# Cross-attention of a fused attention and expert kernel, reassociated: scores from x̂ (Wq Kᵀ), output from P (V Wo)

## The reference

```python
xn  = layernorm(x)
q, k, v = xn @ Wq, ctx @ Wk, ctx @ Wv          # 8 heads of 64, inner width 512
P   = softmax(q k^T * 64**-0.5)                # per head, 256 x 77
x   = x + (P v) @ Wo + bo
h   = layernorm(x)
rw  = routing weights of 16 experts, from h @ normalized sim_matrix, gates, relu, top-2 fallback, softmax
q2, k2, v2 = sum over e of rw[e] * (h @ proj[e])   # 64 wide each, 16 experts
a   = causal softmax(q2 k2^T / 8) v2
out = x + sum over e of rw[e] * (a @ o_proj[e])
```

## Time and profile before

| | |
|---|---|
| median of 3 runs | 2771.4 us (2769.01 to 2772.56) |
| the profiled execution | 2767.65 us, of it a span of 2765.9 us from first to last instruction |
| busy share of the span | PE 98%, PEld 93%, DVE 81%, ACT 44%, POOL 43% |
| granted TensorE clock | 0.992 on average |
| DMA | 113.6 MB, 41 GB/s; the queue's packets take 16.9% of the 16 engines' time |
| chain that ended last | PE 90%, ACT 4%, DVE 2%, issue 2% |

### The profile page before, as it was taken

One profiled execution on the slowest core, in us unless ns is written; L12 is line 12 of the kernel. 1 busy time (PEld: TensorE's weight loads), 2 busy tenths in 40 slices (PEclk: granted clock), 3 DMA queues, 4 the chain that ended last, 5 costly groups with the idle time before them and its releaser, 6 DMA issues.

```text
span 2765.9 us, 65910 instructions
## 1 busy us (share of the span) xinstructions
PE 2698.9 (98%) x19012; PEld 2582.4 (93%) x19012; DVE 2233.7 (81%) x6371; ACT 1226.8 (44%) x4240; POOL 1186.2 (43%) x1739
## 2 busy tenths in 40 slices
PE   5999999999999999999999999999999999999996
PEld 4999999999999999999999999999999999999996
DVE  6788888888888888888888878888888888888875
ACT  4444444444444444544444444444445444444441
POOL 1353443444444444534434434444445344344343
PEclk8999999999999999999999999999999999999998
DMA  4111111111111111111111111211111111111111
GB/s 105 29 46 43 33 44 35 41 44 28 44 48 28 44 44 32 44 44 32 44 39 37 44 28 44 48 28 44 45 32 44 44 32 44 42 34 44 33 39 39
DMA packets 131437, 113.59 MB, mean 41 GB/s; under 512 B 24720, under 2 KB 130640, under 8 KB 131408
## 3 DMA queue, kind: packets, MB, share of 16 engines
q1 hardware_dynamic: 131408, 113.23, 16.9%
HBM read 95.38 MB, written 17.83 MB: 41 GB/s over the span
## 4 chain that ended last, share of the span: by engine, by line
PE 90%; ACT 4%; DVE 2%; issue 2%; POOL 0%; DMA 0%; DVEq 0%; ACTq 0%; SPq 0%; POOLq 0%
PE bank_b L373 12%; PE bank_b L374 11%; PE bank_b L375 11%; PE bank_a L375 10%; PE bank_a L374 10%; PE bank_a L373 10%; PE bank_c L373 5%; PE bank_c L375 5%; PE bank_c L374 5%; PE bank_a L487 4%; PE bank_c L551 1%; PE bank_a L447 1%; PE bank_a L446 1%; PE bank_a L418 1%; DVE k_stack L1011 1%
## 5 line engine op out<-in xcount | busy, mean ns | idle before, releaser
L373 PE MATMUL bank_b<-wqkv_hi,x2T_lo 128*128 128x384 f32 (+1 forms) x2048 | 719.8, 351 | 0.0
L374 PE MATMUL bank_b<-wqkv_lo,x2T_hi 128*128 128x384 f32 (+1 forms) x2048 | 693.8, 339 | 0.0
L375 PE MATMUL bank_b<-wqkv_hi,x2T_hi 128*128 128x384 f32 (+1 forms) x2048 | 688.7, 336 | 0.0
L1000 DVE SCALAR_TENSOR_TENSOR acc<-bank_b,rw,acc 128x192 f32<-128x192 f32 x1792 | 641.1, 406 | 4.9 <-PE bank_b L375 2.4
L1256 POOL TENSOR_TENSOR mixs_lo<-mix,mixs_hi 128x512 fp32r<-128x512 f32 x256 | 380.5, 1517 | 156.4 <-ACT mixs_hi L777 156.4
L373 PEld LDWEIGHTS bank_b<-wqkv_hi,x2T_lo 128*128 128x128 f32 x2048 | 386.1, 189 | 17.6 <-DVE acc L1000 17.2
L374 PEld LDWEIGHTS bank_b<-wqkv_lo,x2T_hi 128*128 128x128 f32 x2048 | 386.2, 189 | 0.0
L375 PEld LDWEIGHTS bank_b<-wqkv_hi,x2T_hi 128*128 128x128 f32 x2048 | 385.2, 188 | 0.0
L1178 POOL TENSOR_TENSOR pow_out<-pow_in,expo 128x2 f32<-128x2 f32 (+1 forms) x128 | 111.7, 873 | 607.6 <-DVE pow_in L862 508.3
L723 ACT ACTIVATE probs<-bank_a,s_max 128x77 f32<-128x77 f32 x1024 | 316.5, 330 | 56.6 <-DVE s_max L931 56.6
L373 PE MATMUL bank_c<-wo_hi,mixs_lo 128*128 128x256 f32 x1024 | 293.8, 287 | 3.7 <-POOL mixs_lo L1256 3.7
(11 more groups left out here) (195 smaller groups left out, 6926.9 us busy)
## 6 DMA issues: line engine op xcount, KB each, us to landing
rw_all<-rw_dram SPq DMA_DIRECT2D x128, 512.0 KB, 5.9
xt<-in_x_dram SPq DMA_DIRECT2D x64, 256.0 KB, 2.7
out_dram<-mix SPq DMA_DIRECT2D x64, 256.0 KB, 2.2
ct<-in_ctx_dram SPq DMA_DIRECT2D x64, 57.8 KB
ct<-in_ctx_dram SPq DMA_DIRECT2D x64, 19.2 KB
mix<-in_L_ffn_o_proj_dram SPq DMA_DIRECT2D x2, 512.0 KB, 4.4
rw_dram<-rwT SPq DMA_DIRECT2D x64, 16.0 KB, 1.4
x_tiles<-in_L_xattn_Wq_dram SPq DMA_DIRECT2D x1, 512.0 KB, 6.8
```

The source lines that it names most:

```text
L373: nc.tensor.matmul(dst, lhs[1], rhs[0], start=start, stop=False)
L374: nc.tensor.matmul(dst, lhs[0], rhs[1], start=False, stop=False)
L375: return nc.tensor.matmul(dst, lhs[0], rhs[0], start=False, stop=stop)
L1000: V.scalar_tensor_tensor(acc[:, t, k, :], src, rw[:, t, e:e + 1], acc[:, t, k, :], ALU.mult, ALU.add).then_inc(b_evac, 1)
```

## The change

Scores: S = xn (Wq Kᵀ). For each head G = Wq_h K_hᵀ (256 channels by 77 keys) is made ahead, and `a_s` multiplies the transposed xn by it; queries are no longer made. Output: y = P (V Wo). For each head U = V_h Wo_h (77 by 256), stacked to 616 rows; the normalized probabilities are transposed as 616 rows (five chunks of at most 128: 10 transposes) and multiplied by U in 30 matmuls; `a_pv` is gone. G and U depend on the context alone. They are made for three batches at once (231 key columns, padded to 232): one `j_ct`, 4 `j_k`, 4 `j_v`, 8 `j_g`, 8 `j_u` per group of three, spread over the three steps of a group by the table JOBS, and are written, hi and lo, to DRAM (`g_dram`, `u_dram`) through two `draft` tiles. Before its use each batch loads its G (128 rows of 9,856 bytes) and its U (616 rows of 2,048 bytes). Batch 0 is a group of its own, made in an opening before the first step; the group of batches 1 to 3 is made in the two steps of index -1 (17 jobs) and in the step of batch 0 (8 jobs).

The loop body is now three steps (r = 0, 1, 2). Several tiles share memory: xn and x2n lie in `probs`, `rwT` in `mix`, k_hi, q_stack, k_stack, v2, p2T in the two pT tiles, aT2 in the qkv part of `late_tiles`. POOL's order of pieces is unchanged. The diff, cut to its core:

```diff
+    A_ORDER = ("E0", "PT0", "PT1", "PT2", "E1", "Y", "E2", "E3", "M1", "XT", "M2", "M3", "S0", "S1", "S2", "S3", "L1", "L2")
+    JOBS = ({"E0": ("v", 2), "E1": ("u", 2), "E2": ("u", 3), "E3": ("v", 3), "M1": ("u", 4), "M2": ("u", 5), "M3": ("u", 6),
+             "L1": ("u", 7)},
+            {"E0": ("ct", 0), "E1": ("k", 0), "E2": ("k", 1), "E3": ("g", 0), "M1": ("g", 1), "M3": ("k", 2), "L1": ("g", 2),
+             "L2": ("g", 3)},
+            {"E0": ("k", 3), "E1": ("g", 4), "E2": ("g", 5), "E3": ("v", 0), "M1": ("g", 6), "M2": ("g", 7), "M3": ("v", 1),
+             "L1": ("u", 0), "L2": ("u", 1)})
...
 SP, new order of a step
+                if on(earlier):
+                    store(earlier)
+                turn((store_u, 2), (None,), (store_g, 4))
+                turn((store_u, 3), (None,), (store_g, 5))
+                turn((None,), (store_g, 0), (None,))
+                if r and on(ahead):
+                    load_u(ahead, q + 1, r)
+                turn((store_u, 4), (store_g, 1), (store_g, 6))
+                turn((store_u, 5), (None,), (store_g, 7))
+                if r == 1 and going(gm + 1):
+                    load_ctx(gm + 1)
+                if on(before):
+                    spread_rw(before)
...
 PE
+            def j_g(gm, f):
+                hc, cc = f // 2, f % 2
...
+                for e in range(2):
+                    dst, w_ = bank_job(gm, "g", f)[:, e * KP:e * KP + keys.stop], wq[:, 2 * hc + e, cc * P:(cc + 1) * P]
+                    nc.tensor.matmul(dst, w_, both[:, hc % 2, e, keys], start=True, stop=False)
+                    last = nc.tensor.matmul(dst, w_, only[:, hc % 2, e, keys], start=False, stop=True)
...
             def a_s(n, j):
+                for cc in range(CC):
+                    last = product(bank_a(f"S{j}")[:, 0:HB * NC].rearrange("p (a b) -> p a b", a=2),
+                                   part(xT, slice(None), cc, slice(t * P, (t + 1) * P)),
+                                   [gq[:, 2 * half:2 * half + 2, cc, k, :] for k in range(2)], cc == 0, cc == CC - 1)
+            def a_pT(n, k):
+                if k == 0:
+                    pe.wait_ge(p_ready, at(2, n, 1))
...
                 do(before, b_qkv, 6)
+                turn("E0", (j_v, 2), (j_ct,), (j_k, 3))
                 do(before, b_qkv, 7)
                 do(earlier, c_y, 0)
                 do(before, b_qkv, 8)
                 do(earlier, c_y, 1)
+                fill("PT0", now, a_pT, 0)
+                fill("PT1", now, a_pT, 1)
                 do(earlier, c_y, 2)
+                fill("PT2", now, a_pT, 2)
                 do(earlier, c_y, 3)
                 do(before, b_qkv, 9)
+                turn("E1", (j_u, 2), (j_k, 0), (j_g, 4))
                 do(before, b_qkv, 10)
+                fill("Y", now, a_y, 0)
                 do(before, b_qkv, 11)
+                turn("E2", (j_u, 3), (j_k, 1), (j_g, 5))
+                do(now, a_y, 1)
                 do(before, b_qkv, 12)
+                turn("E3", (j_v, 3), (j_g, 0), (j_v, 0))
                 do(before, b_qkv, 13)
                 do(before, b_qkv, 14)
                 do(before, b_qkv, 15)
+                turn("M1", (j_u, 4), (j_g, 1), (j_g, 6))
+                fill("XT", ahead, a_xT)
                 do(before, c_rT)
                 do(now, b_xT, 0)
                 do(now, b_xT, 1)
+                turn("M2", (j_u, 5), (None,), (j_g, 7))
                 do(before, c_qk)
                 do(now, b_qkv, 0)
                 do(now, b_qkv, 1)
                 do(before, c_s)
+                turn("M3", (j_u, 6), (j_k, 2), (j_v, 1))
                 do(now, b_qkv, 2)
+                fill("S0", ahead, a_s, 0)
+                fill("S1", ahead, a_s, 1)
+                fill("S2", ahead, a_s, 2)
                 do(before, c_pT)
+                do(now, b_qkv, 3)
                 do(before, c_pv)
+                fill("S3", ahead, a_s, 3)
                 do(now, b_qkv, 4)
+                turn("L1", (j_u, 7), (j_g, 2), (j_u, 0))
                 do(now, b_qkv, 5)
+                turn("L2", (None,), (j_g, 3), (j_u, 1))
...
 ACT, second half of a step
                 do(before, c_qk)
+                turn((j_u, 6), (j_k, 2), (j_v, 1))
                 do(before, c_exp)
                 do(now, b_exp)
+                do(ahead, a_exp, 0)
                 do(before, c_pT)
+                do(ahead, a_exp, 1)
                 do(before, c_pv)
+                do(ahead, a_exp, 2)
                 do(before, c_mix, 0)
+                do(ahead, a_exp, 3)
                 do(before, c_mix, 1)
+                turn((j_u, 7), (j_g, 2), (j_u, 0))
                 do(before, c_mix, 2)
+                turn((None,), (j_g, 3), (j_u, 1))
+                do(before, c_mix, 3)
...
 DVE, second half of a step
+                turn((j_u, 6), (j_k, 2), (j_v, 1))
+                do(ahead, a_s, 0)
                 do(before, c_p)
+                do(ahead, a_s, 1)
                 do(now, b_wsum)
+                do(now, b_qkv, 0)
+                do(ahead, a_s, 2)
                 do(before, c_pT)
                 do(now, b_qkv, 1)
                 do(now, b_qkv, 2)
+                do(now, b_qkv, 3)
                 do(before, c_mix, 0)
+                do(ahead, a_s, 3)
+                do(now, b_qkv, 4)
                 do(before, c_mix, 1)
+                turn((j_u, 7), (j_g, 2), (j_u, 0))
                 do(before, c_mix, 2)
+                turn((None,), (j_g, 3), (j_u, 1))
                 do(before, c_mix, 3)
```

More of the change, by code:

```diff
@@ L360, in _, with step, turn, skip @@
[L360 to L365, removed]
+            load_weights(range(0, 1))
+            load_x(0)
+            load_weights(range(1, 4))
+            load_ctx(1)
+            load_weights(range(4, 6))
+            def step(q, r):
+                ahead, now, before, earlier = [number(q, r) + d for d in (1, 0, -1, -2)]
+                after = number(q, r) + 2
+                gm = group(q, r)
+                def turn(*jobs):
+                    fn, *k = jobs[r]
+                    if fn and going(gm):
+                        fn(gm, *k)
+                def skip():
+                    pass
+                if on(earlier):
[11 more added lines that the diff above has]
+                    spread_rw(before)
+                if on(after) and not (known(after) and after == 0):
+                    load_x(after)
+                turn((store_u, 6), (None,), (None,))
+                if on(after):
+                    load_g(after, *((q + 1, r + 1) if r < 2 else (q + 2, 0)))
+                turn((store_u, 7), (store_g, 2), (store_u, 0))
+                turn((None,), (store_g, 3), (store_u, 1))
+                if not r and on(ahead):
+                    load_u(ahead, q + 1, r)
@@ new lines, in _ @@
+            for hc, pieces in enumerate(((6,), (7, 8), (9,), (10, 11))):
+                store_g(0, 2 * hc)
+                store_g(0, 2 * hc + 1)
+                load_weights(pieces)
+            for hc, pieces in enumerate(((12,), (13,), (), (14, 15))):
+                store_u(0, 2 * hc)
+                load_weights(pieces)
+            step(-1, 1)
+            step(-1, 2)
+            for r in range(3):
+                step(0, r)
+            with sp.Fori(1, LAST) as q:
+                for r in range(3):
+                    step(q, r)
@@ L366, in _ @@
+            for q, r in ENDING:
+                step(q, r)
             sp.wait_ge(y_out, 16 * B)
@@ L503, in a_y @@
[L503 to L511 removed]
+                last.then_inc(xt_fill, 1)
@@ new lines, in j_u @@
+            def j_u(gm, f):
+                hc, tile = f // 2, f % 2
+                weights(gm, W_O)
+                pe.wait_ge(kv_evac, at(H, gm, HC + hc))
+                keys = slice(0, NC) if opened(gm) else slice(tile * TK, (tile + 1) * TK)
+                for e in range(2):
+                    dst, w_ = bank_job(gm, "u", f)[0:keys.stop - keys.start, e * C:(e + 1) * C], wo[:, 2 * hc + e, :]
+                    nc.tensor.matmul(dst, both[:, hc % 2, e, keys], w_, start=True, stop=False)
+                    last = nc.tensor.matmul(dst, only[:, hc % 2, e, keys], w_, start=False, stop=True)
+                last.then_inc(u_fill, 1)
@@ L711, in a_kT @@
[L711 to L717 removed]
+                nc.scalar.activation(hi, stage[k % SLOTS][:, 0:hi.shape[1]], copy).then_inc(wt_hi, 1)
@@ new lines, in stacks, with j_k, j_v @@
+            def stacks(src, k, cols):
+                for e, rows in enumerate((slice(0, D), slice(D, P))):
+                    last = V.tensor_tensor(both[rows, k, e, cols], src[rows, cols], only.bitcast(F32)[rows, k, e, cols], ALU.subtract)
+                last.then_inc(kv_evac, 1)
+            def j_k(gm, hc):
+                dve.wait_ge(kv_hi, at(H, gm, hc))
+                stacks(bank_job(gm, "k", hc), hc % 2, keys(gm))
+            def j_v(gm, hc):
+                dve.wait_ge(kv_hi, at(H, gm, HC + hc))
+                stacks(bank_job(gm, "v", hc), hc % 2, keys(gm))
```

782 lines of the change are left out of this document (461 added, 321 removed).

## The result

The changed kernel takes 3251.1 us (median; 3245.2 to 3257.7) against 2770.8 us: a ratio of 1.173, 95% interval 1.171 to 1.176, so 17% slower. The forecast was 3010 us, range 2790 to 3140. The sign and the kind of cause were right; the time lies outside the range, 241 us above the forecast.

A forecast was written before the change was run, and what follows sets the result against it. PE's instruction stream bounds the kernel at 42.04 us a step; 38.2 of work plus 6.9 of waits gives 45.1. 63 intervals x 3.06 = 193 and 45 of opening on 2765.9 give 3004 of span, 3010 us; range 2790 to 3140.

The forecast's parts named there:

- PE's own work falls by 3.8 us a step: PE's instruction stream: 16.0 us removed and 12.2 added per batch, 0.1 of small gaps gone; 38.2 us per step.
- Wait 1: PE at b3 until the routing lets DVE free b0, T + 7.8 (T: b1 issued); 2.2 us every step, beside 0.5 before c_s.
- Wait 2: PE at b8 until DVE, behind c_mix 3, has read b5; about 1.8 us in two steps of three.
- Wait 3: PE at a_pT 0, which now needs both halves of the probabilities from POOL; 1.4 to 1.7 us.
- Wait 4: PE at c_qk behind b15, DVE's reading and POOL's sum; 1.4 us, bounds 0.5 and 2.
- I leave the clock at 1.00.: TensorE's clock stays at 2.4 GHz because the waits are short; only the upper bound allows for 1.2 GHz.
- I take no cost: rwT's spread on SP behind the store of M2: lands near T + 9 to 10, before c_mix 0 wants it; no cost.
- Rival (c): rw lands late behind the stores on SP, 1.5 us more per step, 3105 us; chance 0.09.
- Opening: Before the first a_y: 46 group jobs at about 1 us, hardly overlapped, add 45 us, bounds 15 and 80.
- rival (a): Chains shorter than laid out, PE stays full, all four waits gone: -197, about 2575 us; chance 0.14.

The follow-up runs named there:

- a8: a4 with the loops of all five engines written out, so that no engine jumps back; 2970.4 us, ratio 1.073.
- a6: a4 with the four POOL operations of the routing's fallback left out (not computed); 3046.6 us, ratio 1.099.
- b1: The kernel before with a_kT and the queries a_q moved on PE ahead of the first b_qkv, by order alone; 3034.1 us, ratio 1.095.
- a3: The changed kernel with ACT doing L1 before c_mix 1, and DVE doing L1 after c_mix 2 and L2 after c_mix 3; 3177.3 us, ratio 1.147.
- E0: Not a run: a job in the changed kernel's step, on PE between b6 and b7; its transposes of xn waited behind an exponential, 1.0 us a step.
- a1: The changed kernel with spread_rw on SP moved ahead of the store of M2, load_ctx and load_u; 3165.2 us, ratio 1.143.
- a12: The changed kernel with only its loops written out on all five engines; 3173.3 us, ratio 1.145.
- a4: The changed kernel with the differences of a1 and a3 together; 3087.3 us, ratio 1.115.
- a9: a8 with three group jobs moved behind c_s on PE, ACT and DVE, and spread_rw ahead of their stores on SP; 3111.0 us, ratio 1.123.
- a10: a9 with one more group job moved ahead of a_pT 0; 3094.8 us, ratio 1.118.
- b2: The kernel before with its one-step loop body written three times on SP, PE, ACT and DVE; 2798.6 us, ratio 1.0096.
- a7: a4 with the loop body of PE, ACT, DVE and SP doubled from three steps to six; 3025.1 us, ratio 1.092.

## Why the forecast was wrong by 241 us

By its own steps:

- **PE's own work falls by 3.8 us a step.** Right in kind, somewhat too large. The changed kernel has 38.7 us of work at full clock in a step, where the kernel before is busy for 41.9, so the fall is 3.2. a8 runs at (2900.6 - 112.4) / 63 = 44.3 us a step: 4.9 idle, an estimated 0.9 of slow clock, 38.4 of work. Which term of the sum was short is open; scores of 308 columns stand 0.14 us apart, as forecast.
- **Wait 1, b3 and c_s.** Right in place and size: 1.9 + 0.3 against 2.2 + 0.5. b0 was freed and b3 started at T + 7.75 in the step from T = 1053.5, forecast T + 7.8. That the routing is what b3 waits for is shown by a6. That a_q was its cover is only argued: b1, which moves a_q, brings a wait of the same size behind DVE's copy of q and none at b3.
- **Wait 2, b8.** The mechanism was right: DVE stood idle before L1 and L2 for 1.15 and 1.14 us, each time for ACT's draft, forecast 1.15. a3 removes most of it and gains 74 us.
- **Wait 3, a_pT.** 0.6 instead of 1.5 in the changed kernel, because PE arrived later, held up by the jump and at E0. When those were gone (a8) it was 1.0. That PE's lateness is the reason is an inference from these two numbers.
- **Wait 4, c_qk.** 1.0 instead of 1.4, inside its bounds. b_xT, 0.6, was missing.
- **"I leave the clock at 1.00."** This is the step that failed most. The forecast put 6.9 us of waits into a step and priced only the waits themselves; about 2.3 us of the 3.57 missing a step are matmuls behind a wait at less than full clock. The upper bound of the range did not allow enough for it.
- **"I take no cost" for rw.** Rival (c) was right and had chance 0.09. The trip of rwT took 4.4 us (median to landing) where it took 1.4 before, and c_mix 0 waited for rw_all in 37 steps; a1 puts the order of SP at 86 us, slow clock included. I had the late departure but no price for landing beside 0.5 MB of stores.
- **The loop body.** Not in the forecast: 59 us of waits in 17 places, 78 us in all (a12), up to 117 once other waits are gone (a8 against a4). The diff showed a loop over q with three steps in its body where there had been one, and I gave that no price.
- **Opening** 56 instead of 45, inside its bounds.
- Two slips without weight: the 129.5 us of the earlier trace rows are 3.08 steps and not three, and rival (a) comes to 45 - 239 = -194, not -197.

The parts add roughly: of 281 us from the changed kernel to a8, order of SP 86, order of c_mix 74, jumps 117. a12 and a8 price the jumps at 78 and 117, so the split depends on the order in which the three are removed. The remaining 200 us to the kernel before are 56 of opening and 2.2 us in each step: 4.7 more idle time, mostly waits 1, 3, 4 and b_xT, and 0.9 of slow clock, less 3.4 of work saved. How far those could be hidden stays open; a9 and a10 are the only orders tried for it.

## To carry to other kernels

Work that looks like the bound may be the cover of a chain on other engines. Before removing it, lay the chain beside what is left, and price each wait that appears in a full TensorE stream at up to twice its length, since the clock can fall behind it. When a change makes a loop's body several times longer, look at the instruction queues and at "issue" just behind the jump; writing the loop out was worth 2 to 4% here. A small transfer on which a chain hangs belongs ahead of bulk stores in its queue.

## What the runs showed of the hardware that was not expected

- A jump back to the start of a body of three steps (about 810 matmuls in the changed kernel, 890 in b2) cost TensorE 1.4 to 1.5 us with little other traffic, and 3.5 to 4.7 us beside the change's stores and loads; with six steps (a7) it was 5.0, at most 6.3, and with a body of one step no such wait is seen. That the instructions are fetched again is inferred from the instruction queues: 4.8 MB in the changed kernel, more than the 3.5 MB of the same kernel without loops (a12), against 0.36 with a body of one step. Where they are held was not tried.
- The clock fell from 2.4 to 1.2 GHz behind waits of 2.14 us in one step of b1 and held behind an equal one in the step before.
- A store of 16 KB behind larger ones landed late: rw_dram, 4.4 us (median) after its issue where it took 1.4 before, and 2.7 in a1, where fewer stores stand ahead of it.
